# Two 64-row matmuls in place of two 128-row ones for the last score pass of a two-layer cross-attention kernel

## What is computed

```python
# layer 0
scores = einsum('bne,bme->bnm', q, k); attn = softmax(scores)
x = q_feat + (attn @ v) @ Wd.T + bd
# layer 1, H = 8
score = einsum('bhqd,bhkd->bhqk', Q, K) / sqrt(256)
ctx = einsum('bhqk,bhkd->bqhd', softmax(score), V)
out = layer_norm(ctx @ Wo + x) * gamma + beta
```

## Time and profile before

| | |
|---|---|
| median of 3 runs | 511.05 us |
| the profiled execution's own time | 510.73 us |
| its span, first to last instruction | 508.90 us |
| TensorE matmul busy | 475.9 us, 94% |
| VectorE busy | 333.3 us, 65% |
| ScalarE busy | 291.6 us, 57% |
| GpSimd busy | 244.1 us, 48% |
| mean granted TensorE clock | 0.994 |

### The profile page before, as it was taken

The page is one execution under the profiler, slowest core; times in us unless marked ns, Lnnn a source line. Parts: engine busy times, 40 slices in busy tenths (PEclk is TensorE's granted clock), DMA queues, the critical chain, the costliest instruction groups (busy, mean ns, idle before and its releaser), DMA issues.

```text
span 508.9 us, 7590 instructions
## 1 busy us (share of the span) xinstructions
PE 475.9 (94%) x2424; PEld 394.5 (78%) x2424; DVE 333.3 (65%) x681; ACT 291.6 (57%) x480; POOL 244.1 (48%) x151
## 2 busy tenths in 40 slices
PE   0989999999979999999999999999999999999992
PEld 0877787777868888888888888888888888788891
DVE  5999866566565658565756585667656765755467
ACT  4667377466565656666556565666556564656222
POOL 4636664455845353637271727263635453353004
PEclk9999999999999999999999999999999999999997
DMA  8413013757756576465656474747484745561002
GB/s 265 137 44 124 1 47 106 235 163 236 229 168 217 176 205 206 166 207 165 206 165 225 146 222 150 243 140 246 141 254 142 236 150 181 167 204 43 0 2 82
DMA packets 53974, 81.97 MB, mean 161 GB/s; under 512 B 5792, under 2 KB 43072, under 8 KB 53824
## 3 DMA queue, kind: packets, MB, share of 16 engines
q1 hardware_dynamic: 44992, 50.16, 34.3%
q10 hardware_dynamic: 8960, 31.54, 16.5%
HBM read 49.16 MB, written 32.51 MB: 160 GB/s over the span
## 4 chain that ended last, share of the span: by engine, by line
PE 72%; DVE 10%; DMA 7%; ACT 5%; issue 2%; POOL 1%; SPq 1%; DVEq 0%; ACTq 0%; POOLq 0%
PE ps_scores L611 25%; PE ps_o L634 6%; PE ps_o L635 5%; PE ps_o L638 5%; PE ps_o L637 5%; PE ps_o L636 5%; DMA probs_t_lo<-scratch 3%; DMA scratch<-probs 3%; PE ps_task L561 2%; PE ps_task L560 2%; PE ps_task L559 2%; PE ps_out L559 2%; DMA ctx_raw<-in_context 2%; ACT probs L975 1%; PE ps_out L561 1%
## 5 line engine op out<-in xcount | busy, mean ns | idle before, releaser
L506 POOL TENSOR_TENSOR probs_t_lo<-probs_t_lo,probs_t_hi 128x1024 fp32r<-128x1024 f32 (+1 forms) x75 | 146.2, 1960 | 180.6 <-ACT probs_t_hi L987 180.4
L987 ACT ACTIVATE probs_t_hi<-probs_t_lo 128x1024 fp32r<-128x1024 f32 (+1 forms) x75 | 64.6, 881 | 44.3 <-DMA probs_t_lo<-scratch 44.2
L634 PE MATMUL ps_o<-probs_t_hi,val_hi 128*128 128x512 f32 (+1 forms) x144 | 56.6, 393 | 2.8 <-DVE o_lo L1356 2.6
L1301 DVE RECIPROCAL row_inv<-row_sum 128x1 f32<-128x1 f32 x72 | 11.4, 160 | 70.6 <-PE ps_scores L611 68.6
L635 PE MATMUL ps_o<-probs_t_lo,val_hi 128*128 128x512 f32 (+1 forms) x144 | 56.6, 393 | 0.0
L638 PE MATMUL ps_o<-probs_t_lo,val_rem 128*128 128x512 f32 (+1 forms) x144 | 56.4, 391 | 0.0
L637 PE MATMUL ps_o<-probs_t_hi,val_rem 128*128 128x512 f32 (+1 forms) x144 | 56.0, 389 | 0.0
L636 PE MATMUL ps_o<-probs_t_hi,val_lo 128*128 128x512 f32 (+1 forms) x144 | 55.9, 388 | 0.0
L1338 DVE STREAM_TRANSPOSE probs<-probs 128x1024 f32<-128x1024 f32 x30 | 37.4, 1245 | 24.8 <-ACT probs L975 24.8
L611 PE MATMUL ps_scores<-key_hi,q_hi 128*128 128x512 f32 x144 | 46.6, 405 | 2.2 <-DVE neg_scores L1314 1.7
L1338 DVE STREAM_TRANSPOSE neg_scores<-neg_scores 128x1024 f32<-128x1024 f32 x30 | 37.2, 1242 | 14.4 <-ACT neg_scores L975 14.4
(11 more groups left out here) (247 smaller groups left out, 1090.3 us busy)
## 6 DMA issues: line engine op xcount, KB each, us to landing
probs_t_lo<-scratch SPq DMA_DIRECT2D x240, 128.0 KB, 3.0
scratch<-neg_scores ACTq DMA_DIRECT2D x30, 512.0 KB, 3.3
scratch<-probs ACTq DMA_DIRECT2D x30, 512.0 KB, 3.8
ring<-in_weights_a SPq DMA_DIRECT2D x9, 512.0 KB, 5.2
ring<-in_weights_b SPq DMA_DIRECT2D x9, 512.0 KB, 6.0
ring<-in_keys_t SPq DMA_DIRECT2D x4, 512.0 KB, 3.4
ctx_raw<-in_context SPq DMA_DIRECT2D x2, 768.0 KB, 9.1
ring<-in_context SPq DMA_DIRECT2D x16, 96.0 KB, 2.7
```

The source lines that it names most:

```text
L506: nc.gpsimd.tensor_tensor(pt_lo[b][:, t, k, :], pt_lo[b][:, t, k, :].bitcast(f32), moved_part(j, k).bitcast(f32), ALU.subtract).then_inc(m ...
L634: pe.matmul(o0, val_hi[b][:, kt, :], hi, start=first, stop=False)
L987: act.activation(moved_part(j, k), pt_lo[b][:, t, k, :].bitcast(f32), ACT.Copy)\
```

## The change

The last score pass (query's rest by the keys' rounded part, 64 features) becomes one matmul of 64 rows for each bank. For keys 0 to 511 it uses array rows 0 to 63, for keys 512 to 1023 rows 64 to 127. For that the rounded part of the second bank's keys has to lie in rows 64 to 127: in `key_rem`, columns 512 to 1023, the two parts trade places (the 128-row pass 4 does not notice, as the query's rounded part stands in both halves). And `q_lo[b][:, 1, :]` holds the query's rest in both halves in place of zeros: where VectorE wrote 64 rows from PSUM it writes 128, and `split_folded` has a second instruction. GpSimd's two clears and TensorE's wait for them go; GpSimd's remainder split becomes two instructions of 512 columns for one of 1024.

```diff
+def low_rows(half):
+    return slice(REM, P) if half == 0 else slice(0, REM)
+def high_rows(half):
+    return slice(0, REM) if half == 0 else slice(REM, P)
...
-                lo = key_rem[b][REM:P, :]
                 pool.wait_ge(piece_hi, HI_OF[k + 1])
...
-                nc.gpsimd.tensor_tensor(lo, ring[(k + 1) % 2][REM:P, :], lo.bitcast(f32), ALU.subtract)\
-                    .then_inc(piece_split, 1)
+                first, second = (key_rem[b][low_rows(half), half * BANK:(half + 1) * BANK] for half in range(2))
+                nc.gpsimd.tensor_tensor(first, ring[(k + 1) % 2][low_rows(0), 0:BANK], first.bitcast(f32),
+                                        ALU.subtract)
+                nc.gpsimd.tensor_tensor(second, ring[(k + 1) % 2][low_rows(1), BANK:2 * BANK], second.bitcast(f32),
+                                        ALU.subtract).then_inc(piece_split, 1)
...
-            for b in range(BATCHES):
-                nc.gpsimd.memset(q_lo[b][REM:P, 1, :].bitcast(f32), 0.0).then_inc(rest_cleared, 1)
-                pool.wait_ge(rest_cleared, b + 1)
...
                 passes = ((q_hi[b][:, 0, q], key_hi[b]), (q_hi[b][:, 0, q], key_lo[b]),
-                          (q_lo[b][:, 0, q], key_hi[b]), (q_hi[b][:, 1, q], key_rem[b]),
-                          (q_lo[b][:, 1, q], key_rem[b]))
+                          (q_lo[b][:, 0, q], key_hi[b]), (q_hi[b][:, 1, q], key_rem[b]))
...
+                if task is not None:
+                    pe.wait_ge(task_free, task + 2)
+                for half in range(2):
+                    n, rows_of = slice(half * BANK, (half + 1) * BANK), high_rows(half)
+                    last = pe.matmul(ps_scores[:, n], q_lo[b][rows_of, 1, q], key_rem[b][rows_of, n],
+                                     start=False, stop=True)
                 last.then_inc(scored, 1)
...
             def split_queries(task, b, m, layer):
-                kept = slice(0, REM if m else P)
-                hi = q_hi[b][kept, m, :].bitcast(f32)
+                hi = q_hi[b][:, m, :].bitcast(f32)
...
             def split_folded(b, folds):
                 dve.wait_ge(folded_hi, 2 * folds + 2)
-                dve.tensor_tensor(q_lo[b][0:REM, 1, :], rem_sum[0:REM, :], q_hi[b][0:REM, 1, :].bitcast(f32),
-                                  ALU.subtract).then_inc(folded, 1)
+                hi = q_hi[b][0:REM, 1, :].bitcast(f32)
+                dve.tensor_tensor(q_lo[b][0:REM, 1, :], rem_sum[0:REM, :], hi, ALU.subtract)
+                dve.tensor_tensor(q_lo[b][REM:P, 1, :], rem_sum[0:REM, :], hi, ALU.subtract).then_inc(folded, 1)
```

More of the change, by code:

```diff
@@ L274, in build @@
         vals0_hi = sem("vals0_hi")
-        rest_cleared = sem("rest_cleared")
         vals0_split = sem("vals0_split")
@@ L604, in scores @@
                             pe.wait_ge(task_hi, hi_before(task) + (1 if i == 0 else 2))
-                        if i in (2, 4):
-                            pe.wait_ge(task_free, task + (1 if i == 2 else 2))
+                        if i == 2:
+                            pe.wait_ge(task_free, task + 1)
                     if keys is not None and i == 3:
@@ L610, in scores @@
                         n = slice(half * BANK, (half + 1) * BANK)
-                        last = pe.matmul(ps_scores[:, n], left, right[:, n],
-                                         start=(i == 0), stop=(i == len(passes) - 1))
+                        pe.matmul(ps_scores[:, n], left, right[:, n], start=(i == 0), stop=False)
+                if task is not None:
[4 more added lines that the diff above has]
+                                     start=False, stop=True)
                 last.then_inc(scored, 1)
@@ L785, in _ @@
             pe.wait_ge(chunk_split, CHUNKS)
-            pe.wait_ge(rest_cleared, BATCHES)
             scores(-1, 0, task=T_Q0)
@@ L1382, in split_queries @@
                 dve.wait_ge(task_hi, hi_before(task) + 1)
-                kept = slice(0, REM if m else P)
-                hi = q_hi[b][kept, m, :].bitcast(f32)
+                hi = q_hi[b][:, m, :].bitcast(f32)
                 if layer:
-                    dve.tensor_tensor(q_lo[b][kept, m, :], task_bank(task)[kept, :], hi, ALU.subtract)\
-                        .then_inc(task_free, 1)
+                    dve.tensor_tensor(q_lo[b][:, m, :], task_bank(task)[:, :], hi, ALU.subtract).then_inc(task_free, 1)
                 else:
-                    dve.scalar_tensor_tensor(q_lo[b][kept, m, :], task_bank(task)[kept, :], vec[kept, m:m + 1], hi,
+                    dve.scalar_tensor_tensor(q_lo[b][:, m, :], task_bank(task)[:, :], vec[:, m:m + 1], hi,
                                              ALU.add, ALU.subtract).then_inc(task_free, 1)
@@ L1467, in split_chunk @@
                 else:
-                    dve.tensor_tensor(key_rem[b][REM:P, n], src[REM:P, 0:BANK], key_rem[b][REM:P, n].bitcast(f32),
+                    rows_of = low_rows(half)
+                    dve.tensor_tensor(key_rem[b][rows_of, n], src[rows_of, 0:BANK], key_rem[b][rows_of, n].bitcast(f32),
                                       ALU.subtract).then_inc(chunk_split, 1)
@@ L1604, in split_task @@
                     b, m = (1, j) if j < 2 else (0, j - 4)
-                    kept = slice(0, REM if m else P)
-                    dve.tensor_tensor(q_lo[b][kept, m, :], bank[kept, :], q_hi[b][kept, m, :].bitcast(f32),
+                    dve.tensor_tensor(q_lo[b][:, m, :], bank[:, :], q_hi[b][:, m, :].bitcast(f32),
                                       ALU.subtract).then_inc(task_free, 1)
```

## The result

The change makes the kernel slower: 524.75 us median of 4 runs (523.62 to 525.87) against 511.24 us of the kernel before in the same comparison, a ratio of 1.0248 with a 95% interval of 1.0214 to 1.0283. That is 13.5 us, where I had forecast 6.6 us less. It is inside the range on record, close to its upper end, and on the other side of the forecast.

The account below looks back on a forecast made before the run. TensorE was taken to bound over half the span: 0.231 us saved less 0.11 a tile, 0.12 by 55 tiles, takes 6.6 from 510.73 to 504.1 us; with 0.32 for the median, 504.5. Range 497 to 525.

Parts of the forecast that it names:

- What bounds the kernel, and how many tiles count: TensorE sets the time over more than half of the span; 55 of the 72 score tiles count.
- The pair runs side by side: Last score pass: its two matmuls on different array halves take one step, saving at most 0.231 us a tile.
- I take 0.11 us a tile: one uncovered weight load: Cost of both shape changes around a tile's last pass, chosen from a range of 0 to 0.54 us.
- the restart of the array: Trace row after an idle array: first matmul pair 0.11 or 0.12 us longer, for a weight load nothing hid.
- The rule that I had set against the trace: Trainium skill's tiling page: going from one tiling mode to another drains the engine; no trace row could confirm it.
- the array empties at each change of shape: Rival, start and end of each last pass: 516 to 517.5 us, tail alone (chance 0.23); 528 to 533 with reload (0.18).
- three signs of that rival: Pair over 0.23 us after pass 4's last matmul, next work over 0.39 us after the pair, tile 2.40 to 2.62.
- Cost 0; if the cover were gone, at most 0.60 us once a head in step 2, 4 us: `split_folded`'s second VectorE instruction, 14 of some 0.60 us, would fit into VectorE waits of 0.96 and 0.72 us.
- 128 rows for 64 in the other writes of `q_lo`: 692 against 683 ns. Nothing.: VectorE's wider writes of the query's rest would take about as long as before and cost nothing.
- GpSimd's split in two and the clears: Ahead of head 0's key use: split 0.2 us longer, twice; two 0.52 us clears go; no effect on the total.
- The slack of 0.20 us for `o_lo`: TensorE's wait before `values`, twice a head: a saving of 0.12 fits, one of 0.231 would lose 0.4 us.
- A measurement of this kernel can tell about 0.2%, 1 us: Smallest difference from no change that a measurement was taken to show.

Follow-up runs that it names:

- early_pairs: Changed kernel with the 64-row pair only in the 16 tiles of layer 0 and head 0, 128-row matmuls in the other 56; 516.35 us, ratio 1.0115.
- same_side: Kernel before with both matmuls of the last pass on rows 0 to 63, so no overlap is possible; 533.35 us, ratio 1.0395.
- pair_twice: Changed kernel with the 64-row pair of the last pass issued twice in each tile; 537.28 us, ratio 1.0531.
- pair_only: Kernel before with only the last pass's matmuls changed to the 64-row pair, leaving out a product for keys 512 to 1023; 520.39 us, ratio 1.0153.
- early_wide: Kernel before with one edit: `split_queries` writes 128 rows of the query's rest where it wrote 64; 514.11 us, ratio 1.0055.
- no_second: Changed kernel with its last pass over 128 rows and without `split_folded`'s second instruction; 512.8 us, ratio 1.0043.

## Why the prediction was wrong

**What bounds the kernel, and how many tiles count: right.** TensorE's own steps set the time from head 1 on. I counted 55 tiles; 52 lie behind tile 11 and seven of eight grow, which makes about 45, and `early_pairs` shows that the first 16 cost about 0.1 us. The count was a fifth too high, which alone would have cost little. It is no constant either: where a tile loses more, more of the tiles count (by the medians `same_side` lost 20.8 us at 0.42 a tile, about 50 tiles).

**The pair runs side by side: right**, 0.231 us a tile saved (`pair_twice`: 0.23 us for a further pair of matmuls; `same_side`: 0.23 us more without it). The 6.6 us that I had added up from it came out as 7.8 us lost (`pair_only`).

**"I take 0.11 us a tile: one uncovered weight load": this is the step that failed.** The range that I had bounded was 0 to 0.54 us for two changes; it is 0.41. The 0.11 us load is uncovered at both changes, not at one in sum, and on top the array empties. I chose by the row I found the nearest, the restart of the array, and then applied it once, with the argument that two loads might just fit into a step. They never had to: at a change the loader does not run ahead at all. The loads start with their matmul, behind 0.36 and 0.25 us in which the loader was idle. So the two changes cost 0.41 us and not 0.11, and the sum changes its sign: 0.231 - 0.41 is a loss of 0.18 us a tile where I had a gain of 0.12. The rule that I had set against the trace was right. By the Trainium skill, page "TensorEngine Tiling (Array Packing)", section "Key Properties", changing the tiling mode drains TensorE, and this chip does it at each change, in both directions.

**The rival "the array empties at each change of shape": right in mechanism.** Its price was 0.16 us of tail and 0.11 of reload, 0.54 a tile; measured are about 0.10 and 0.11, 0.41 a tile. The recorded tail of a matmul (0.39 less 0.23) overstates what is lost when nothing overlaps it. Two of the three signs of that rival are there: the pair comes more than 0.23 us behind pass 4's last matmul (which by one step starts at 315.95 and so 0.33 us ahead of it), and the next work more than 0.39 behind the pair. The third, a tile of 2.40 to 2.62 us, is just missed as the prediction counts it: 2.38 us from its start to the next work. With the 0.11 us that the next work's own late load adds it is 2.49. Worked with the measured numbers: (0.41 - 0.23) x 45 = 8 us, which is `pair_only`'s 7.8.

**"Cost 0; if the cover were gone, at most 0.60 us once a head in step 2, 4 us": a second step that failed.** I named the idle time that hides VectorE's second instruction, and it is there, 0.96 and 0.72 us. What I did not ask is what runs on GpSimd at the moment at which the instruction now starts. Held for 2.8 us it does not fit into 0.96. The 3.3 us come from one to four events of 1.1 to 2.3 us each in the executions profiled, not from 14 small ones, so the size agrees with the bound that I gave by chance only.

**"128 rows for 64 in the other writes of `q_lo`: 692 against 683 ns. Nothing.": wrong in effect, right in duration.** The write is as long as before, and yet it costs 2.8 us through VectorE's sums, held by GpSimd near 54 us, and in some executions through the clock that falls behind the gap. The trace of before shows the one addition of 2.22 us, where GpSimd is held and not VectorE, but nothing in it says that the write would turn this round.

**GpSimd's split in two and the clears: nothing to be seen** apart from that; `early_wide` has neither and costs no less than `no_second`, which has both.

**The slack of 0.20 us for `o_lo`:** not tested by a slower TensorE. The waits for it are 2.5 us in four, where they were 2.6 in three.

**"A measurement of this kernel can tell about 0.2%, 1 us": too fine.** Beside the experiments single runs of the kernel before took 509.1 to 514.2 us, and the intervals of the ratios are 0.2 to 0.5% either way.

## What to carry to other kernels

A change between 128-row and 64-row matmuls cost about 0.205 us here, on average over both directions, and comes in pairs. Two 512-column matmuls side by side save 0.23 us, so a 64-row stretch has to save two such steps before it pays; pack many small matmuls behind one another, or leave one pass at 128 rows with zeros, as the kernel before does. That a longer stretch does pay was not tried here: `pair_twice`, with two such pairs, just about breaks even, and the rest follows from 0.23 us for each further pair.

An instruction that VectorE's idle time hides by its length may still collide with GpSimd: when it reads two SBUF operands or is a fast copy, look up what GpSimd starts just ahead of it (0.01 to 0.42 us in these traces), and price the event at GpSimd's duration.

## What was unexpected in the hardware

- 96 of 128 rows cost no change of shape (ratio 1.0001), 64 of 128 do.
- Four changes of shape a tile cost twice what two cost (0.79 to 0.83 us against 0.41 to 0.43), and the weight loader stands idle ahead of both, the one in and the one out (0.36 and 0.25 us).
- A VectorE copy of 0.42 us was held for 2.58 us by a GpSimd subtraction of 2.38 us, just as the instruction with two SBUF inputs was.
- A write with more rows and the same length of 0.74 us was enough to turn four VectorE sums from 0.41 to 0.95 us and one GpSimd addition beside them from 2.22 to 0.84 us, with the same 0.17 to 0.18 us between their starts.
- Behind 3 us in which TensorE was busy for 0.91 (`early_wide`: 1.05) the granted clock was 0.52 and 0.53 for 3 us, and in other executions with the same wait it stayed at 1.00. It cost 1.3 to 1.6 us at tile -3 (`no_second`, `early_wide`).
